# Accumulating DMAs for five of eight batches; the last three batches' residual added on GpSimd and VectorE

## The reference, cut to what matters

```
x = x + tanh(g_xattn) * attention(layernorm(x), ctx, ctx)          # "x2" below
y = ffn(layernorm(x))      # quantised input and weights; silu(gate) * up; quantised again; down
return x + tanh(g_ffn) * y
```

## Time and profile before

| | us |
|---|---|
| median of 3 runs | 284.72 |
| lowest, highest | 281.92, 285.21 |
| profiled execution, its own time | 283.28 |
| its span | 281.5 |
| attention and weights done, x scale known (line 1024 ends) | 218.0 |
| h scale known (line 1088 ends) | 256.0 |
| last DMA issue begins (line 411) | 276.52 |

### The profile page before, as it was taken

How to read it: one execution, slowest core, us unless ns; L and a number is a source line. 1 busy time by engine, 2 the same in 40 slices (tenths; PEclk the granted TensorE clock), 3 DMA queues, 4 the chain that set the end, 5 groups by cost and what they waited for, 6 DMA issues and landing times.

```text
span 281.5 us, 6092 instructions
## 1 busy us (share of the span) xinstructions
PE 231.6 (82%) x1752; PEld 156.1 (55%) x1756; DVE 214.7 (76%) x463; ACT 174.4 (62%) x326; POOL 126.1 (45%) x203
## 2 busy tenths in 40 slices
PE   1699979989979999999998999999872488863980
PEld 1587858868646756656575666755540233322650
DVE  3469976979968697797969779799317479997992
ACT  1326466466667667775777767676941488865950
POOL 3375555543441435445373534539505153330363
PEclk9999979999999999999999999999987599997896
DMA  7829779988355445545243555000000700000199
GB/s 234 250 52 311 231 241 263 240 225 222 115 159 112 108 79 115 113 113 107 65 104 65 113 113 114 2 1 4 3 2 2 261 0 1 0 0 2 21 131 148
DMA packets 31638, 31.28 MB, mean 111 GB/s; under 512 B 5248, under 2 KB 28288, under 8 KB 31616
## 3 DMA queue, kind: packets, MB, share of 16 engines
q1 hardware_dynamic: 26832, 27.87, 38.2%
q0 software_dynamic: 1904, 1.84, 5.1%
q10 hardware_dynamic: 2880, 1.31, 1.8%
HBM read 20.65 MB, written 10.22 MB: 110 GB/s over the span
## 4 chain that ended last, share of the span: by engine, by line
PE 40%; DVE 18%; issue 12%; DMA 10%; ACT 6%; POOL 6%; SPq 3%; DVEq 1%; POOLq 1%; ACTq 0%
PE bank_o L1305 7%; PE bank_a L1288 6%; PE bank_b L1275 5%; PE bank_m L1331 5%; DMA x_rows<-in_x 4%; PE bank_a L1194 4%; PE bank_b L1431 3%; DMA big<-max_parts 3%; PE bank_m L1313 2%; DVE neg_max L806 2%; DVE arena L1096 2%; PE bank_o L1203 2%; DMA big<-in_ctx 2%; DVE h_max L1056 2%; ACT wgu_rows L766 1%
## 5 line engine op out<-in xcount | busy, mean ns | idle before, releaser
L806 DVE TENSOR_REDUCE neg_max<-bank_b 128x2 f32<-128x512 f32 x128 | 83.8, 680 | 14.8 <-PE bank_b L1275 11.3
L660 ACT ACTIVATE big<-bank_a 128x512 f32<-128x512 f32 x128 | 69.8, 588 | 16.0 <-PE bank_a L1288 15.3
L1288 PE MATMUL bank_a<-big 98*128 98x256 bf16 x256 | 49.0, 274 | 3.5 <-DMA big<-max_parts 2.6
L1275 PE MATMUL bank_b<-big 96*128 96x256 bf16 x224 | 42.8, 272 | 0.0
L1305 PE MATMUL bank_o<-big,v_cur 128*32 128x256 f32 x512 | 34.3, 385 | 0.8 <-ACT big L660 0.8
L1194 PE MATMUL bank_a<-arena,w_t 128*128 128x256 f32 x128 | 33.1, 408 | 0.6 <-DVE resid L817 0.5
L477 POOL CAST max_parts<-max_f 8x256 bf16<-8x256 f32 x16 | 6.4, 403 | 52.3 <-issue 49.8
L1288 PEld LDWEIGHTS bank_a<-big 98*128 98x128 bf16 x256 | 21.1, 97 | 13.6 <-ACT big L660 3.0
L1194 PEld LDWEIGHTS bank_a<-arena,w_t 128*128 128x128 f32 x128 | 25.3, 207 | 4.7 <-DVE resid L817 1.0
L450 POOL TENSOR_TENSOR arena<-resid,arena 128x512 bf16<-128x512 f32 x16 | 18.3, 1159 | 12.1 <-ACT arena L600 12.1
L1275 PEld LDWEIGHTS bank_b<-big 96*128 96x128 bf16 x224 | 21.5, 97 | 3.2 <-issue 0.2
(11 more groups left out here) (158 smaller groups left out, 434.8 us busy)
## 6 DMA issues: line engine op xcount, KB each, us to landing
qk_parts<-arena SPq DMA_DIRECT2D x8, 768.0 KB, 4.8
big<-qk_parts SPq DMA_DIRECT2D x32, 192.0 KB, 3.7
big<-qk_parts SPq DMA_DIRECT2D x32, 128.0 KB, 3.9
x_rows<-in_x SPq DMA_DIRECT2D x8, 256.0 KB, 5.2
big<-qk_parts SPq DMA_DIRECT2D x32, 64.0 KB, 3.9
out<-x_rows SPq DMA_DIRECT2D x8, 256.0 KB, 3.1
big<-in_ctx SPq DMA_DIRECT2D x7, 256.0 KB, 5.2
out<-v_all POOLq DMA_DIRECT2D x7, 256.0 KB, 4.4
```

Of the source, the lines that this page charges most:

```text
L660: act.activation(p_buf[:, h % HH], bank_a[:, h % 2].rearrange("p (c s) -> p c s", c=QC), ACT.Exp, scale=SCALE).then_inc(exp_done, 1)
L806: dve.tensor_reduce(neg_max[:, p, :, h], bank.rearrange("p (c s) -> p c s", c=QC), axis=AX.X, op=ALU.max, negate=True).then_inc(max_done, 1)
L1275: done = mm(to, q_st[0:KR, p, h, c * P:(c + 1) * P], k_st[0:KR, p, h], start=True, stop=not masked)
L1288: done = mm(to, k_st[0:KM, p, h, k * P:(k + 1) * P], q_st[0:KM, p, h], start=True, stop=not masked)
```

## The change

A constant `ONTO = 5` splits the batches. Batches 0 to 4 stay as they were: early store of x2, accumulating DMA later. Batches 5 and 6 are no longer stored early; GpSimd, after its five accumulating DMAs, adds `v_all` to `x_rows` in SBUF (`row_sum`), and SyncE stores the sums. Batch 7 is added by VectorE as before, but in two instructions of one tile each; SyncE stores the first tile, and ScalarE's queue issues the store of the second, on a semaphore of its own that it then waits for.

```diff
--- before.py
+++ after.py
@@ -86,6 +86,7 @@
     NCH = 4
     CW = T // NCH
     CT = CW // P
+    ONTO = 5
 
 
 
@@ -265,7 +266,7 @@
         pad_zero, h_scale_ready = sem("pad_zero"), sem("h_scale_ready")
         y_rounded, y_free, hq_ready = sem("y_rounded"), sem("y_free"), sem("hq_ready")
         down_done, y_scaled, x2_stored = sem("down_done"), sem("y_scaled"), sem("x2_stored")
-        out_last, summed = sem("out_last"), sem("summed")
+        out_last, summed, row_sum, stored_act = sem("out_last"), sem("summed"), sem("row_sum"), sem("stored_act")
         dve_chain, pool_chain = sem("dve_chain"), sem("pool_chain")
 
 
@@ -404,13 +405,17 @@
             step(7, 1, ahead=False, after=False)
 
             sp.wait_ge(scale_ready, 1)
-            for b in range(B - 1):
+            for b in range(ONTO):
                 sp.wait_ge(x2_done, b + 1)
                 sp.dma_start(out_dram[:, tiles(b)], x_rows[:, tiles(b)]).then_inc(x2_stored, 16)
+            for b in range(ONTO, B - 1):
+                sp.wait_ge(row_sum, b - ONTO + 1)
+                sp.dma_start(out_dram[:, tiles(b)], x_rows[:, tiles(b)]).then_inc(stored, 16)
             sp.wait_ge(out_last, 1)
-            sp.dma_start(out_dram[:, tiles(B - 1)], x_rows[:, tiles(B - 1)]).then_inc(stored, 16)
-            sp.wait_ge(stored, 16)
-            sp.wait_ge(summed, 16 * (B - 1))
+            sp.dma_start(out_dram[:, T // P - 2], x_rows[:, T // P - 2]).then_inc(stored, 16)
+            sp.wait_ge(stored, 16 * (B - ONTO))
+            sp.wait_ge(stored_act, 16)
+            sp.wait_ge(summed, 16 * ONTO)
 
 
         @block.gpsimd
@@ -554,10 +559,14 @@
                     if n == 0 and m == 0:
                         pool.wait_ge(xq_ready, 2)
                         over_scale(3)
-            pool.wait_ge(x2_stored, 16 * (B - 1))
-            for b in range(B - 1):
+            pool.wait_ge(x2_stored, 16 * ONTO)
+            for b in range(ONTO):
                 pool.wait_ge(y_scaled, b + 5)
                 pool.dma_start(out_dram[:, tiles(b)], v_all[:, tiles(b)], accum_op=ALU.add).then_inc(summed, 16)
+            for b in range(ONTO, B - 1):
+                pool.wait_ge(y_scaled, b + 5)
+                pool.tensor_tensor(x_rows[:, tiles(b)], x_rows[:, tiles(b)], v_all[:, tiles(b)], ALU.add
+                                   ).then_inc(row_sum, 1)
 
 
         @block.scalar
@@ -765,6 +774,9 @@
                     act.wait_ge(y_free, t + 1)
                     act.activation(h_round[:, q], h_all[:, :, bass.ds(t * P, P)], ACT.Identity,
                                    scale=INV_H, bias=magic[:]).then_inc(y_rounded, 1)
+            act.wait_ge(out_last, 2)
+            act.dma_start(out_dram[:, T // P - 1], x_rows[:, T // P - 1]).then_inc(stored_act, 16)
+            act.wait_ge(stored_act, 16)
 
 
         @block.vector
@@ -1127,8 +1139,8 @@
             scale_down(B - 1)
 
             dve.wait_ge(y_scaled, B + 4)
-            dve.tensor_tensor(x_rows[:, tiles(B - 1)], x_rows[:, tiles(B - 1)], v_all[:, tiles(B - 1)], ALU.add
-                              ).then_inc(out_last, 1)
+            for t in range(T // P - 2, T // P):
+                dve.tensor_tensor(x_rows[:, t], x_rows[:, t], v_all[:, t], ALU.add).then_inc(out_last, 1)
 
 
         @block.tensor
```

## The result

The changed kernel takes 280.44 us, median of 22 runs (278.92 to 283.22). The kernel before takes 282.56 us, median of 22 runs now (280.39 to 285.21), 2.2 us less than the three runs that stood ahead of the prediction had as their median. The ratio is 0.9925, 95% interval 0.9903 to 0.9948: 2.1 us faster, 1.5 to 2.7. The interval doesn't reach 1, so the gain is more than noise, and it is far from 2%. The profiled execution took 279.81 us, its span is 278.0.

The account below looks back on a forecast made before the run. VectorE's pace bounds the last stage to some 274 us, then the DMA engines. Last landing moves from 281.0–281.05 to 279.65, a 1.4 us gain: 284.0 - 1.4 = 282.6 us, range 280.7 to 285.2.

Parts of the forecast that it names:

- the middle of the four: Level of the kernel before, 284.0 us, taken from four runs spread over 3.29 us; the 1.4 us gain was subtracted from it.
- (1): From 218 us on, two early stores (512 KB) go; nothing waits for them, so counted as nothing.
- (2): At the end, two accumulating DMAs go, 4.06 us of the DMA engines, and two plain stores come, 1.56 us.
- (3): At the end, GpSimd adds batches 5 and 6, 1.27 us each, the second ending at 276.65.
- (4): SyncE stores batch 5 at 275.45, batch 6 at 276.7; batch 7's first tile waits behind until 277.1.
- (5): VectorE's two half sums of batch 7, 0.4 us each, delayed by GpSimd's second add; tiles ready at 276.9 and 277.3.
- The sum's 1.56 us of packets: Stores of batches 6 and 7 at the end: 512 KB, 544 packets at 0.046 us over 16 engines, 1.56 us.
- The rival of slow plain packets: Plain stores as slow as accumulating packets, 0.120 us: batches 6 and 7 land at 282.2, 1.1 us slower; chance 0.02.
- GpSimd's DRAIN: Kernel's end: taken to wait for the last accumulating landing; rival: fixed time behind GpSimd's last instruction, no gain, 284.0; chance 0.10.
- Slower through stretched adds: GpSimd's two adds take 2.53 us each and delay SyncE's last store: 0.75 us slower, 284.8; chance 0.05.
- Full overlap of the stores: No port meeting, last stores on two queues each land in 2.2 us, at 278.9: gain 2.1 us, 281.9; chance 0.12.

Follow-up runs that it names:

- the GpSimd part alone: Changed kernel, but batch 7 added by VectorE in one instruction and stored by SyncE in one DMA; tail 4.03 us, ratio to before 0.994.
- the sum from PSUM: Changed kernel with batch 7 scaled in place in PSUM and its half sums reading it there; tail 4.04 us, ratio to before 0.9917.
- tile 14 ahead of batch 6: Kernel with the sum from PSUM, SyncE's stores reordered to batch 5, tile 14, batch 6; tail 3.73 us, ratio to before 0.9918.
- four accumulating DMAs: Changed kernel with ONTO = 4, so GpSimd also adds batch 4; tail 4.42 us, ratio to before 0.9957.
- the halves alone: Kernel before with seven accumulating DMAs kept, batch 7 added in two halves and stored on two queues; tail 5.28 us, ratio to before 0.9968.
- Batch 6 not accumulated: Kernel before without batch 6's accumulating DMA, its y missing from the output; tail 4.08 us, one execution, no ratio.

## Why the prediction was wrong

The direction, the mechanism and the place hold; the time, 280.44 us, fell below the range by 0.26 us. The step that failed is the last of the sum: "I set the time against 284.0, the middle of the four". Over 22 runs the kernel before has its median at 282.56, and 282.56 - 1.4 = 281.2 would have been inside. Three runs with 3.3 us of spread gave no better level than that, and I drew the range's lower end only 1.2 us under the middle, where the level lay 1.44 under it. The second, smaller miss is the gain: 1.4 us forecast, 2.1 (1.5 to 2.7) timed. Together they are the 2.16 us between 282.6 and 280.44. The tail says where: with the change it was predicted at 279.65 - 275.77 = 3.88 and is 4.01 and 4.06. But the tail before was taken at 5.28 ("Before it was 281.0 to 281.05"), the shortest of four profiles with the mean 5.73. 5.73 - 4.03 = 1.7 us is the gain at the end, and it lies within the timed interval.

Point by point, in us behind the last scaling, predicted and then measured in the first profile after:

| | predicted | measured |
|---|---|---|
| store of batch 5 issued | -0.32 | -0.41 |
| GpSimd's second add ends | 0.88 | 0.79 |
| store of batch 6 issued | 0.93 | 0.82 |
| tile 14 issued | 1.33 | 1.23 |
| tile 15 issued | 1.53 | 1.44 |
| last landing | 3.88 | 4.01 |

- (1) Early stores at nothing: held by the run that keeps them all, as far as one profile tells.
- (2) Accumulating DMAs as the load: held. The run without batch 6's DMA takes 1.2 to 1.9 us off, the GpSimd part alone gives the whole gain in the tail, and the halves add nothing to it (4.01 and 4.06 with them, 4.03 without).
- (3) GpSimd's add at 1.27: 1.25 measured.
- (4) Tile 14 behind batch 6 on SyncE's queue: held, and worth 0.3 us at most, once the tiles are ready sooner.
- (5) VectorE held up by GpSimd's add: shown by the sum from PSUM, 0.76 us beside 1.38. The Trainium skill's rule ("SBUF — State Buffer", "Who interferes with whom") that two SBUF inputs contend with a GpSimd instruction that reads SBUF agrees with these runs. Taken away alone it left the tail as it was, 4.04; with tile 14 ahead of batch 6 the tail was 3.73.
- The sum's 1.56 us of packets were right: plain packets in the changed kernel came at

```profile
q1 hardware_dynamic: 523, 0.49, 60.9%
q10 hardware_dynamic: 143, 0.13, 16.3%
```

  over 2.4 us (274.5 to 276.9), (0.609 + 0.163) x 2.4 x 16 / (523 + 143) = 0.0445 us each against 0.046. The rival of slow plain packets, at 0.120, is out with it. The last store was issued 0.09 us sooner behind the last scaling than forecast and landed in 2.57 us where the sum had 2.35: that is the 0.13 us by which the tail was missed.
- GpSimd's DRAIN: it ended 0.26 us behind the landing of its last DMA and 3 us before the kernel's end, where a fixed time behind the last instruction would have put it 4.5 us behind 274.28. That rival is out.
- Slower through stretched adds: not in this kernel, but with four accumulating DMAs an add did take 2.51 us, beside VectorE's rounding and clipping: a stretch of the size that the rival named.
- Full overlap of the stores (a gain of 2.1 through landings in 2.2 us): the stores did land in 2.1 to 2.6 us, but the tail is 4.01 and not 278.9 - 275.77 = 3.1. With the sum from PSUM and tile 14 ahead, the issues were as this rival has them (tile 15 at 0.82 and batch 6 at 0.88 behind the last scaling), and the tail was still 3.73, as batch 6 took 2.85 us to land. So it is out; that the timed gain is also 2.1 is a coincidence of the longer tails before.

What stays open: why the accumulating DMAs' end varies by 0.7 us from profile to profile, and what makes the stretches of the same work before it vary (until the weights' scale 55.0 to 58.1 us, from there to the x scale 158.5 to 161.8, to the h scale 38.0 to 39.7), with and without the change. No run tried it. It is of the size of the 4 to 5 us between the fastest and the slowest run of a kernel. Chips may have a part in it: the two longest tails of before are from one chip, but the run of before and the halves alone, both of another, show 5.68 and 5.28. Batch 6 not accumulated was profiled on a chip for which there is no profile of before, so its 1.2 to 1.9 us rests on tails from elsewhere. Whether the 0.4 us between the timed 2.1 and the tail's 1.7 is more than noise can't be told either.

## What to carry to other kernels

When the last thing is a DMA, count what the DMA engines still have to move behind the last computed value, and price each kind of transfer by its packets' time: here an accumulating packet costs 2.6 plain ones, so adding in SBUF and storing once is cheaper at the end, while in the middle, where the DMA engines are partly idle (shares of 0.41 and 0.66 from 260 to 270), the accumulating DMAs cost nothing that the profiles show: VectorE's pace stayed the same with seven, five and four. Measure such a change from the last common event to the end, in several profiles of both kernels; one profile's tail was 0.45 us off its mean and three runs' median 2.2 us off that of 22, for a gain of 2.1. And give an addition beside GpSimd's an operand in PSUM where there is one: it frees VectorE sooner, by 0.62 us here, and whether the kernel gains depends on what stands behind it.

## What the runs showed of the hardware

- A VectorE addition with two SBUF inputs waits for a running GpSimd addition: 128x256 took 1.04 us and 128x512 1.31 us, ending 0.28 and 0.55 us behind it; alone they take 0.41 and 0.69. With one input in PSUM 128x256 takes 0.42 beside it.
- The other way round, VectorE's rounding and clipping held a GpSimd add from 1.25 to 2.51 us and lost nothing themselves.
- An accumulating DMA of 256 KB to HBM takes 2.03 us of packet time on each of the 16 DMA engines, a plain one 0.78. Packet times can overlap on an engine: the share reaches 1.16.
- GpSimd's DRAIN at the end lasts until 0.26 us behind the landing of its last DMA (0.34 before), here 4.5 us behind its last instruction before and 0.69 after. With four accumulating DMAs, which had landed 2.2 us before its last add ended, it ended 0.43 us behind that add.
- From h's scale to the last scaling the stage took 19.77 to 19.79 us in all fourteen profiles, whether seven, six, five or four accumulating DMAs stood in the queue.
